# Values and gates from one product of 288 columns, ahead of the units, in the projection stage of an attention and mixture-of-experts layer

## The reference, cut to what matters

```python
q = split_heads(hidden_states @ Wq.T + bq)          # 8 x 1024 tokens, width 256, 16 heads of 16
k = split_heads(hidden_states @ Wk.T + bk)
v = split_heads(hidden_states @ Wv.T + bv)
proj = split_heads(hidden_states) @ gru_W.T + gru_b
gates = sigmoid(proj.reshape(B, H, N, 2, 4).sum(-1))
gate_out = gates[..., 0:1] * (gates[..., 1:2] * gru_const - 1.0) + 2.0
scores = q @ k.T * scale + gate_out * pos_bias      # softmax, times v, times Wo
```

## Time and profile before

| | |
|---|---|
| median of 3 runs | 3342.86 us (3342.19 to 3348.31) |
| profiled execution, its own time | 3342.88 us |
| its span, first to last instruction | 3341.1 us |
| busy in the span: PE, DVE, ACT, POOL | 93%, 71%, 62%, 46% |
| mean granted clock of TensorE | 0.968 |
| `project` | 0 to some 263 us, 8% of the span |
| `attend` | 263 us to some 2040 us |

### The profile page before, as it was taken

The page is one execution under the profiler, slowest core; times in us unless marked ns, Lnnn a source line. Parts: engine busy times, 40 slices in busy tenths (PEclk is TensorE's granted clock), DMA queues, the critical chain, the costliest instruction groups (busy, mean ns, idle before and its releaser), DMA issues. The chain is left out here.

```text
span 3341.1 us, 58394 instructions
## 1 busy us (share of the span) xinstructions
PE 3099.0 (93%) x18893; PEld 2035.0 (61%) x18893; DVE 2384.1 (71%) x5688; ACT 2060.6 (62%) x4106; POOL 1522.6 (46%) x1916
## 2 busy tenths in 40 slices
PE   7986999999999999999999996875999999999991
PEld 4553555555555555554555553764888888888881
DVE  6877899989898899998999893775444443444436
ACT  3546999999999999998999993211322232232230
POOL 3444444444444444444444440003666666666650
PEclk9997999999999999999999998987999999999995
DMA  6883232333333232324232323534776667677666
GB/s 225 280 276 96 49 69 56 64 66 63 58 58 66 63 67 51 66 50 78 51 67 51 68 46 115 177 115 152 225 218 208 213 213 219 208 226 219 207 215 208
DMA packets 274612, 436.24 MB, mean 131 GB/s; under 512 B 58538, under 2 KB 202996, under 8 KB 255636
## 3 DMA queue, kind: packets, MB, share of 16 engines
q1 hardware_dynamic: 233108, 370.94, 39.9%
q0 software_dynamic: 30464, 44.94, 6.3%
q10 hardware_dynamic: 10752, 16.78, 1.3%
HBM read 325.60 MB, written 106.42 MB: 129 GB/s over the span
## 5 line engine op out<-in xcount | busy, mean ns | idle before, releaser
L837 DVE CUSTOM_DVE_ANT_0 tot<-sc,gbias 128x1024 f32<-128x1024 f32 x1024 | 1240.0, 1211 | 27.0 <-POOL gbias L698 26.7
L698 POOL TENSOR_SCALAR gbias<-slab_a,gs 128x484 f32<-128x484 f32 x1024 | 687.6, 673 | 867.4 <-DVE negm L837 847.1
L891 ACT ACTIVATE probs<-tot,negm 128x640 f32<-128x640 f32 (+2 forms) x1024 | 767.3, 749 | 41.6 <-DVE negm L837 33.5
L1465 ACT ACTIVATE f_hid<-f_ph,f_w_up 128x256 f32<-128x256 f32 (+1 forms) x584 | 268.5, 460 | 666.1 <-PE f_ph L1424 657.6
L740 PE MATMUL sc<-ks,qs 120*128 120x512 bf16 x2048 | 615.8, 382 | 38.5 <-PEq L207 22.4
L849 DVE COPY wt<-pb 128x256 f32<-128x256 f32 (+1 forms) x1024 | 398.1, 389 | 169.4 <-PE pb L761 168.9
L1424 PE MATMUL f_ph<-f_xt,f_w_up 128*128 128x256 f32 (+1 forms) x2336 | 484.6, 366 | 1.5 <-DVE f_xt L1484 1.2
L1436 PE MATMUL f_py<-f_w_down,f_hid 128*128 128x256 f32 x2176 | 481.6, 379 | 0.0
L916 ACT ACTIVATE wt<-pa 128x256 f32<-128x256 f32 (+1 forms) x1024 | 447.8, 437 | 43.2 <-PE pa L752 29.3
L752 PEld LDWEIGHTS pa<-ident,probs 128*128 128x128 f32 x2560 | 330.0, 140 | 227.8 <-issue 98.2
L1424 PEld LDWEIGHTS f_ph<-f_xt,f_w_up 128*128 128x128 f32 x2336 | 421.1, 191 | 55.6 <-issue 2.7
(11 more groups left out here) (203 smaller groups left out, 3171.3 us busy)
## 6 DMA issues: line engine op xcount, KB each, us to landing
f_w_down<-in_w_down SPq DMA_DIRECT2D x73, 1152.0 KB
f_w_up<-in_w_up SPq DMA_DIRECT2D x73, 1028.0 KB
ks<-k_d SPq DMA_DIRECT2D x192, 128.0 KB, 5.0
qs<-q_d SPq DMA_DIRECT2D x384, 64.0 KB
v_d<-vt SPq DMA_DIRECT2D x16, 1024.0 KB, 6.2
vs<-v_d SPq DMA_DIRECT2D x32, 512.0 KB, 6.8
rcb<-rc_d SPq DMA_DIRECT2D x64, 256.0 KB
q_d<-parts SPq DMA_DIRECT2D x32, 384.0 KB, 3.2
```

The costliest lines, as they stand in the source:

```text
L698: pool.tensor_scalar(gbias[x % NG][:, SIDE:SIDE + BAND], slab[:, hh, :], gs[u % 2][:, i, hh:hh + 1], 1.0, ALU.mult, ALU.mult).then_inc(gbi ...
L837: dve.tensor_tensor_reduce(tot[x % 2][:], sc[:, x % 2, :], gbias[x % NG][:, w:w + N], -1.0, 3.0e38, ALU.add, ALU.min, negm[h % 2][:, c:c + ...
L891: act.activation(probs[x % 2][:, 0:hi - lo], tot[x % 2][:, lo:hi], ACT.Exp, bias=negm[h % 2][:, c:c + 1], scale=-1.0).then_inc(near_done, 1)
```

## The change

- Values and gates become one product: `w_vg` holds the 256 columns of the values and the 32 of the gates side by side (288). `pv` has three banks in place of two and takes `pg`'s place; a block of 128 tokens `t` goes to bank `t % 3`. Block 3 goes to bank 0 again and waits for `gl_read` 4h + 1, which ACT sends after block 0's sigmoids.
- These products stand at the start of the half, ahead of the units, and no longer behind the transposes.
- DVE reads the values first in each half, right behind the slab of the half before and ahead of its wait for `low_done`.
- ACT does eight sigmoids of 128x16 in place of two of 128x64, each pair behind DVE's reading of that block (`v_read`).
- SP stores the values of a half ahead of its input load, which waits for the units now, and both ahead of the q, k and far stores.
- The 11 small constants are issued by ACT, in a new order, at the start.
- `c_ind` lies in a part of `slab` and the four copies into `ks_0` are made in half 2, between the rest of the far unit and the slab.

```diff
-        pv = es.enter_context(nc.psum_tensor("pv", [P, 2, 2, E], F32))
-        pg = es.enter_context(nc.psum_tensor("pg", [P, 4, 2, H], F32))
+        pv = es.enter_context(nc.psum_tensor("pv", [P, 3, 512], F32))
...
             def load(b, s):
 
                 if not isinstance(b, int) or b > 0:
-                    sp.wait_ge(v_done, 4 * b + 2 * s - 2)
+                    sp.wait_ge(unit_done, 8 * b + 4 * s - 4)
                 sp.dma_start(xt[:, s], ...).then_inc(x_loaded[s], 16)
+
+            def store_v(b, s):
+                sp.wait_ge(v_read, (2 * b + s + 1) * 4)
+                sp.dma_start(v_d[...], vt[:, s] ...).then_inc(stored[s], 16)
...
             with sp.Fori(0, B - 1) as b:
                 for s in range(2):
+                    store_v(b, s)
                     load(b + 1, s)
                     store(b, s)
...
@@ block.tensor
                     pe.wait_ge(x_loaded[s], 16 * (b + 1))
-                    pe.wait_ge(gl_read, 2 * h)
+                    pe.wait_ge(gl_read, 4 * h)
                     for t in range(4):
+                        if t == 3:
+                            pe.wait_ge(gl_read, 4 * h + 1)
                         for c in range(EC):
-                            mm = pe.matmul(pg[:, t] ..., xt[:, s, c, t * P:(t + 1) * P], gate_wt[:, c] ..., ...)
-                    mm.then_inc(gl_done[s], 1)
+                            mm = pe.matmul(pv[:, t % 3, 0:E + 2 * H], xt[:, s, c, t * P:(t + 1) * P], w_vg[:, c, :], ...)
+                        mm.then_inc(v_done, 1)
                     pe.wait_ge(qk_full, NU * h)
...
                     mm.then_inc(gates_turned, 1)
-                    pe.wait_ge(v_read, 4 * h)
-                    for t in range(4):
-                        for c in range(EC):
-                            mm = pe.matmul(pv[:, t // 2, t % 2, :], xt[...], w_v[:, c, :], ...)
-                        if t % 2 == 1:
-                            mm.then_inc(v_done, 1)
 
@@ block.scalar
+            for to, of in small:
+                act.dma_start(to, of).then_inc(small_in, 16)
...
-                    act.wait_ge(gl_done[s], b + 1)
                     act.wait_ge(g_step, 2 * h)
-                    for g in range(2):
-                        act.activation(gsig[:, g], pg[:, :, g, :], ACT.Sigmoid, bias=gate_bs[:, g:g + 1]).then_inc(gl_read, 1)
+                    for t in range(4):
+                        act.wait_ge(v_read, 4 * h + t + 1)
+                        act.activation(gsig[:, 0, t], pv[:, t % 3, E:E + H], ACT.Sigmoid, bias=gate_bs[:, 0:1])
+                        act.activation(gsig[:, 1, t], pv[:, t % 3, E + H:E + 2 * H], ACT.Sigmoid, bias=gate_bs[:, 1:2]).then_inc(gl_read, 1)
                     act.wait_ge(stored[s], 16 * STORES * b)
 
@@ block.vector
+                    dve.wait_ge(stored[s], 16 * STORES * b)
+                    for t in range(4):
+                        dve.wait_ge(v_done, 4 * h + t + 1)
+                        dve.tensor_tensor(vt[:, s, t, :, 0:D], pv[:, t % 3, 0:E] ..., b_v[:] ..., ALU.add).then_inc(v_read, 1)
                     dve.wait_ge(low_done, h * NS)
                     for u in range(NU):
...
                     rest_of(NU - 1)
-                    dve.wait_ge(stored[s], 16 * STORES * b)
-                    for t in range(4):
-                        dve.wait_ge(v_done, 2 * h + t // 2 + 1)
-                        dve.tensor_tensor(vt[:, s, t, :, 0:D], pv[:, t // 2, t % 2, :] ..., b_v[:] ..., ALU.add).then_inc(v_read, 1)
-
                     dve.wait_ge(gates_turned, h + 1)
...
                     rest_of(NU)
+
+                    if h == 2:
+                        for hh in range(4):
+                            dve.tensor_copy(ks_0[96:128, hh, :], ind).then_inc(consts_set, 1)
+                        dve.wait_ge(consts_set, 4)
```

More of the change, by code:

```diff
@@ L227, in project @@
         mask_h = sb("mask_h", [P, EC, H])
-        gate_wt = sb("gate_wt", [P, EC, 2, H])
         gate_bs = sb("gate_bs", [P, 2])
@@ L231, in project @@
         b_qk = sb("b_qk", [P, 2, EC])
-        w_v = sb("w_v", [P, EC, E])
+        w_vg = sb("w_vg", [P, EC, E + 2 * H])
         b_v = sb("b_v", [P, E])
@@ L260, in project @@
         summed, far_part, gates_set = sem("summed"), sem("far_part"), sem("gates_set")
-        small = [(onehot[:], a["c_onehot"]), (rel[:], a["rel"]), (gw[:], a["gru_w"]), (gb[:], a["gru_b"]),
-                 (mask_h[:], a["c_mask_h"].rearrange("k p n -> p k n")),
+        ind = slab[96:128, 12:16, :].rearrange("p h n -> p (h n)")[:, 0:N]
+        small = [(gw[:], a["gru_w"]), (mask_h[:], a["c_mask_h"].rearrange("k p n -> p k n")),
                  (far_mask[:], a["c_far"].rearrange("k p n -> p k n")),
-                 (full[96:128, 0:2, :].rearrange("p u n -> p (u n)"), a["c_ind"]),
+                 (gb[:], a["gru_b"]), (onehot[:], a["c_onehot"]), (rel[:], a["rel"]), (ind, a["c_ind"]),
                  (ends[:], a["ends"]), (far_ends[:], a["far_ends"]), (ident[:], a["c_ident"]), (fill[:], a["c_fill"])]
         weights = [(w_qk[:, 0], a["wq"].rearrange("(c p) n -> p c n", p=P)), (w_qk[:, 1], a["wk"].rearrange("(c p) n -> p c n", p=P)),
-                   (w_v[:], a["wv"].rearrange("(c p) n -> p c n", p=P)), (b_qk[:, 0], a["bq"]), (b_qk[:, 1], a["bk"]),
+                   (w_vg[:, :, 0:E], a["wv"].rearrange("(c p) n -> p c n", p=P)), (b_qk[:, 0], a["bq"]), (b_qk[:, 1], a["bk"]),
                    (b_v[:], a["bv"]), (gc_h[:], a["gc_h"])]
@@ L279, in load @@
                 if not isinstance(b, int) or b > 0:
-                    sp.wait_ge(v_done, 4 * b + 2 * s - 2)
+                    sp.wait_ge(unit_done, 8 * b + 4 * s - 4)
                 sp.dma_start(xt[:, s], a["xt"][bass.ds(b, 1), :, s * HT:(s + 1) * HT].rearrange("o (c p) n -> p (o c) n", p=P)).then_inc(x_loaded[s], 16)
+            def store_v(b, s):
+                t0 = s * HT
+                sp.wait_ge(v_read, (2 * b + s + 1) * 4)
+                sp.dma_start(v_d[bass.ds(b * N + t0, HT), :].rearrange("(k p) n -> p k n", p=P),
+                             vt[:, s].rearrange("p k h d -> p k (h d)")).then_inc(stored[s], 16)
             def store(b, s):
@@ L300, in _ @@
             load(0, 1)
-            with nc.allow_non_contiguous_dma(reason="small constants, once"):
-                for to, of in small:
-                    sp.dma_start(to, of).then_inc(small_in, 16)
             sp.wait_ge(line_copied, 1)
@@ L319, in _ @@
             first_batch(sp)
-            store(B - 1, 0)
-            store(B - 1, 1)
+            for s in range(2):
+                store_v(B - 1, s)
+                store(B - 1, s)
             for s in range(2):
@@ L348, in _ @@
                     pe.wait_ge(x_loaded[s], 16 * (b + 1))
-                    pe.wait_ge(gl_read, 2 * h)
+                    pe.wait_ge(gl_read, 4 * h)
                     for t in range(4):
+                        if t == 3:
+                            pe.wait_ge(gl_read, 4 * h + 1)
                         for c in range(EC):
-                            mm = pe.matmul(pg[:, t].rearrange("p g h -> p (g h)"), xt[:, s, c, t * P:(t + 1) * P],
-                                           gate_wt[:, c].rearrange("p g h -> p (g h)"), start=c == 0, stop=c == EC - 1)
-                    mm.then_inc(gl_done[s], 1)
+                            mm = pe.matmul(pv[:, t % 3, 0:E + 2 * H], xt[:, s, c, t * P:(t + 1) * P], w_vg[:, c, :], start=c == 0, stop=c == EC - 1)
+                        mm.then_inc(v_done, 1)
                     pe.wait_ge(qk_full, NU * h)
@@ L364, in _ @@
                     mm.then_inc(gates_turned, 1)
-                    pe.wait_ge(v_read, 4 * h)
-                    for t in range(4):
-                        for c in range(EC):
-                            mm = pe.matmul(pv[:, t // 2, t % 2, :], xt[:, s, c, t * P:(t + 1) * P], w_v[:, c, :], start=c == 0, stop=c == EC - 1)
-                        if t % 2 == 1:
-                            mm.then_inc(v_done, 1)
         @block.scalar
         def _(act):
+            with nc.allow_non_contiguous_dma(reason="small constants, once"):
+                for to, of in small:
+                    act.dma_start(to, of).then_inc(small_in, 16)
             act.wait_ge(loaded, 16 * len(weights))
@@ L408, in _ @@
             for g in range(2):
-                dve.tensor_scalar(gate_wt[:, :, g, :], mask_h[:], wsum[:, g:g + 1], None, ALU.mult)
+                dve.tensor_scalar(w_vg[:, :, E + g * H:E + (g + 1) * H], mask_h[:], wsum[:, g:g + 1], None, ALU.mult)
             dve.tensor_scalar(far_t[:], far_mask[:, 0, :], far_ends[:, 0:1], None, ALU.mult).then_inc(far_part, 1)
@@ L413, in _ @@
                                      op0=ALU.mult, op1=ALU.add).then_inc(gates_set, 1)
-            for hh in range(4):
-                dve.tensor_copy(ks_0[96:128, hh, :], full[96:128, 0:2, :].rearrange("p u n -> p (u n)")).then_inc(consts_set, 1)
-            dve.wait_ge(consts_set, 4)
             dve.wait_ge(loaded, 16 * len(weights))
```

(7 more changed lines are left out.)

6 lines of the change are left out of this document (removed).

## The result

The changed kernel takes 3407.96 us (median of 4 runs, 3407.32 to 3409.0); beside it on the same chip the kernel before took 3345.41 (4 runs, 3342.19 to 3348.31). The ratio is 1.0188, its 95% interval 1.017 to 1.0205: the change costs some 62.6 us. The profiled execution of after has a span of 3405.9 us against 3341.1, a mean granted clock of 0.958 against 0.968, and its own time is 3407.65.

The account below looks back on a forecast made before the run. Bound: a chain through DVE, PE close behind. Thirteen halves 203.8, table load 4.7, clock 26.7, copies 2.7, less 177.8 before, give +60.1; start -2.3 and end +3.5 make +61.3: 3404 us, range 3366 to 3426.

Parts of the forecast that it names:

- The new chain: In each half of the loop, DVE, ACT, PE and DVE again follow one another; a half takes 15.7 us.
- S to F: From the end of DVE's slab operations (S) to the start of its first unit read (F): 4.05 us, before 1.18.
- F to S: From DVE's first unit read to the end of its next slab operations: 11.64 us.
- The signs named for "wrong": DVE still waiting for POOL ahead of its units, two units read 0.67 us apart, or halves under 13.7 us.
- The clock: PE's idle 4.5 us before block 3 halves its clock afterwards: 2.05 us a half, 26.7 for 13 halves.
- The rival in which the clock stays up: Same chain of engines in each half, but PE's idle time costs no clock: 3373 us, chance 0.2.
- Table load: ACT's load ahead of block 0's sigmoids in even halves, now on the path: 0.78 us each, 4.7 for six.
- The copies: Moved into half 2, on DVE's chain with a wait behind them: +2.7 us.
- The start: Constants issued by ACT land 2.5 us earlier; first half's slab end shifts by -2.3 us, ends 0 and -4.2.
- The end: From POOL's last part of half 13 to `attend`: 47.8 us against 44.3 before, +3.5.
- The gates' store: DVE's 1.64 us wait for it ahead of `gtok`, in every second half, goes away.

Follow-up runs that it names:

- the kernel with the added products: Changed kernel with four unread products of 512 columns in PE's idle time ahead of the fourth value block, in most halves: 3377.56 us.
- the kernel with the merge undone: Kernel before, separate products, with the small constants issued by ACT and DVE's wait for POOL's low parts split by unit: 3334.07 us, ratio 0.997.
- the repaired kernel: Changed kernel, copies ahead of the loop, blocks 0 to 2 read early, own semaphore for values' store, POOL wait split by unit: 3325.28 us, ratio 0.9936.

## Why the prediction was right

The forecast was 3404 us, +61.3; measured are +64.8 between the profiled spans and +62.6 between the medians. Point by point:

- *The new chain.* S to F predicted 4.05, measured 3.92 where the clock stays up; F to S predicted 11.64, measured 11.98; the half 15.90 for 15.7. Unit reads 1.65 apart (1.71 predicted). The signs named for "wrong", units 0.67 apart or a wait for POOL ahead of them, are absent. The reason is shown by undoing it: with early reading the 64 us are gone and 18 more. Copies and table loads left the path with it, but by their own experiments they are 2.3 to 4.5 and 6.7 us of these 82.
- *Inside F to S one term was missed and another was too large.* `gtok` starts while POOL is on its three low parts (before, the values' readings stood between) and takes 1.38 for 0.41; from the far unit's end to the end of its rest that is 0.5 a half. The rest of F to S was 0.2 shorter than reckoned. I moved the readings and did not ask what then runs beside POOL.
- *The clock.* Predicted 2.05 a half from the one gap in `merge`, 26.7 over 13 halves. On the path it is 27.4: the stage's 13 halves took 242.8 us (last slab operation of half 0 ends at 37.71, that of half 13 at 280.50), less 13 x 15.90 = 206.7, less table load and copies, 8.7. That is 2.1 a half. The 27.6 of the experiment count other halves (14 and 15 with them, 1 and 3 without), so the halves have to be compared: from the slab of half 3 to that of half 13 it takes 163.2 us with the added products and 184.2 without, 2.1 a half again. So the size was right, but the shape was not that of the earlier trace rows: there the clock fell in the gap and came back 4.3 us after PE resumed; here in an odd half it falls after PE has resumed and is back within some 4 us. The rival in which the clock stays up (3373) falls; the kernel with the added products is nearly that case, at 3377.56.
- *Table load.* Predicted 0.78 an even half; PE's idle time grows by 5.28 - 4.43 = 0.85. It starts right behind ACT's last middle part and doesn't wait for block 0's reading, as taken. With one load left of eight the stage is 6.7 us shorter, with the slightly shorter gaps also in it.
- *The copies.* Predicted 2.7. They took 3.46 beside POOL against 2.50, and PE's idle time in the half behind them is 8.05 against 4.43: 3.6. Mis-sized for the same reason as `gtok`.
- *The start.* Predicted -2.3; the last slab of half 0 ends 2.6 earlier (37.71 against 40.30). The constants landed 1.3 earlier and not 2.5. The first unit was read at 25.74 all the same, 0.6 ahead of the middle of 24.5 to 28.1, since PE did the first four units in 7.03 and not in 9.93. The near hit is luck.
- *The end.* From POOL's last part of half 13 to `attend` it is 327.5 - 281.65 = 45.9 us, predicted 47.8, before 44.3. The last two halves took 37.2 for 36.2, and from POOL's last part to `attend` it was 8.7 for 11.4: SP's issue and the landing were too large by 2.7.
- *The gates' store.* DVE no longer waits ahead of `gtok`, as predicted. In the kernel with the merge undone that wait is back, 1.95 us.

Sum against the prediction, over S of half 0 to S of half 13: chain 206.7 (203.8), clock 27.4 (26.7), table load 5.1 (4.7), copies 3.6 (2.7), in all 242.8 (237.9); the start -2.6 (-2.3) and the end +1.6 (+3.5). The clock's term in this list is what is left over, but by the half it agrees with the experiment made for it. No term is wrong by more than 3 us, and part of the closeness of the whole is that +2.9 for the chain and -1.9 for the end cancel.

## What to carry to other kernels

When a product is moved ahead of others on one engine, look for where its bank is read in the reader's own program: three banks for four blocks mean that everything behind the fourth block waits for that reading, and moving the block (as tried) gave back only half, since the reader keeps its place and the wait that is left still brings the clock down. Put the reading where the product is ready, then move the product; the same merge was 1.9% slower with the late reading and, with the early reading and the wait for POOL's low parts split, 0.6% faster. And price an idle gap of PE twice, once as waiting and once as the clock behind it: here 28 of 64 us.

## What the runs showed of the hardware

- **Small DVE operations wait for most of a POOL operation.** Some 1 us more each time, beside one of about 1.2 us: `gtok` (128x16) 1.38 against 0.41 for four, the slab's two 1.30 against 0.40, the copies 3.46 against 2.50, each beside a running `parts` operation of POOL; DVE's readings from PSUM don't (`vt`, one block: 0.42 alone, 0.41 in the repaired kernel with POOL's operation from 124.07 beside it). The Trainium skill's page "SBUF — State Buffer" (Who interferes with whom) says that GpSimd and DVE share one pair of SBUF ports, held as an exclusive lock for a whole instruction when DVE runs in a two-port mode or has two SBUF inputs; these rows agree with it.
- **The clock after a gap.** Gaps of 4.4 us and more brought it to 1.2 GHz in each of 15 halves. From fourth block to transposes it took 9.4 to 11.0 us where it takes 7.94 with the clock up (the kernel with the added products), some 32 us more over the 15. Gaps of 3.48 us (the fourth block behind the units) brought it down in most halves and left it up in four. Gaps of 1.9 us and less left it at 2.4 GHz (1.00 from 120 to 240 us in the kernel with the added products). Near 2 us both were seen: behind a gap of 2.02 us near the end of the stage, in the kernel before with the constants on ScalarE, it was 0.50 from 236 to 238 us, and behind one of 2.06 in the kernel before it stayed up. The Trainium skill's "TensorE: Matmul & The Clock Gate" (HAM oscillation) describes such a kernel that starts each burst cold. The trace agrees that every such gap is paid for; but in the odd half shown the burst began at full clock and it fell some 0.7 us later. Four products that nobody reads, put into the gap, kept the clock up.
- **A table load adds its own 1.28 us and no more.** It ended at 134.68 and the sigmoid began at 134.69. The Trainium skill's "ScalarE: Activation LUTs" (What ACT_TABLE_LOAD costs) adds a drain of about 1.38 us to each switch; no load in these traces shows one, and the measurement decides.
